# Half-width one-hots in two halves of a bank, a ring of seven pairs for gathered rows, and a reordered opening

## The reference, cut to what matters

```
xn  = layernorm(x)
msg = relu(xn[src] + edge_attr @ W_edge + b_edge)        # 50000 x 256
agg = segment_sum(msg, dst, 3125)                        # dst is sorted
h   = (1 + eps) * xn + agg
g   = relu(batchnorm(relu(h @ W1 + b1) @ W2 + b2))
m   = linear_attention(xn; Wq, Wkv, Wproj)               # elu+1 features, 8 heads
x   = x + g + m
x   = x + mixture_of_experts(layernorm(x))               # 8 experts, top 2
```

## Time and profile before

| | us |
|---|---|
| time, median of 3 (lowest to highest) | 1177.69 (1177.09 to 1181.65) |
| span of the profiled execution (first to last instruction) | 1050.8 |
| what lies around the span, median less span | 126.9 |
| PE busy, share of the span | 964.7, 92% |
| DVE busy | 671.7, 64% |
| ACT busy | 513.5, 49% |
| POOL busy | 555.1, 53% |
| first and last gather issued | 44.2 and 545.8 |

### The profile page before, as it was taken

One profiled execution on the slowest core, in us unless ns is written; L12 is line 12 of the kernel. 1 busy time (PEld: TensorE's weight loads), 2 busy tenths in 40 slices (PEclk: granted clock), 3 DMA queues, 4 the chain that ended last, 5 costly groups with the idle time before them and its releaser, 6 DMA issues.

```text
span 1050.8 us, 17977 instructions
## 1 busy us (share of the span) xinstructions
PE 964.7 (92%) x5112; PEld 810.3 (77%) x5113; DVE 671.7 (64%) x1274; ACT 513.5 (49%) x1036; POOL 555.1 (53%) x627
## 2 busy tenths in 40 slices
PE   5898999999999999999998961799999999999994
PEld 4677888888888888877775860778888888888884
DVE  5455565656655565578886778666666666666663
ACT  3644555555454545455554566444444444444442
POOL 3277777777777777777760040224253353444442
PEclk8899999999999999999998986899999999999998
DMA  9667788788888878998762028412545636635321
GB/s 246 197 154 237 255 267 253 250 268 266 260 254 262 269 247 267 278 313 270 239 202 86 26 89 316 181 26 40 204 90 174 220 50 213 192 73 160 98 38 21
DMA packets 85472, 198.30 MB, mean 189 GB/s; under 512 B 19785, under 2 KB 37139, under 8 KB 84378
## 3 DMA queue, kind: packets, MB, share of 16 engines
q1 hardware_dynamic: 55926, 131.60, 36.1%
q0 software_dynamic: 28752, 64.45, 25.5%
q10 hardware_dynamic: 724, 1.42, 0.5%
HBM read 147.86 MB, written 49.97 MB: 188 GB/s over the span
## 4 chain that ended last, share of the span: by engine, by line
POOL 29%; PE 29%; DMA 19%; issue 13%; DVE 7%; ACT 2%; POOLq 1%; SPq 0%; DVEq 0%; ACTq 0%
POOL work L758 29%; DMA out<-work,rowc 11%; PE banks L1141 6%; PE banks L1166 4%; DMA work<-token_table,tokc 4%; PE banks L470 3%; PE banks L446 3%; PE banks L1168 2%; PE banks L969 2%; PE banks L1054 2%; PE banks L1151 2%; DMA work<-in_edge_attr 1%; PE banks L1042 1%; DMA wts<-in_src 1%; DVE st L1776 1%
## 5 line engine op out<-in xcount | busy, mean ns | idle before, releaser
L758 POOL DMA_INDIRECT work<-node_table,srcT x391 | 379.5, 971 | 157.0 <-issue 117.6
L470 PE MATMUL banks<-work 128*128 128x256 f32 x780 | 179.1, 379 | 1.1 <-issue 1.1
L446 PE MATMUL banks<-w_edge,eaT 128*128 128x256 f32 x780 | 179.3, 380 | 0.0
L470 PEld LDWEIGHTS banks<-work 128*128 128x128 f32 x780 | 148.0, 190 | 21.8 <-issue 1.8
L446 PEld LDWEIGHTS banks<-w_edge,eaT 128*128 128x128 f32 x780 | 143.4, 191 | 16.8
L1166 PE MATMUL banks<-wsplit,hidT_hi 128*128 x416 | 153.3, 408 | 2.1 <-DVE hidT_lo L1908 2.1
L529 DVE TENSOR_TENSOR work<-banks,work 128x512 f32<-128x512 f32 x195 | 126.8, 682 | 26.1 <-DMA work<-node_table,srcT 15.2
L1141 PE MATMUL banks<-wsplit,xeT_hi 128*128 x416 | 134.3, 404 | 2.8 <-DVE xeT_lo L1915 2.8
L483 ACT COPY wts<-banks 128x256 f32<-128x256 f32 x66 | 24.6, 372 | 228.8 <-PE banks L470 227.8
L811 POOL DMA_INDIRECT out<-work,rowc x52 | 83.4, 1605 | 82.2 <-ACT work L1441 45.6
L1168 PE MATMUL banks<-wsplit,hidT_lo 128*128 x416 | 116.8, 281 | 0.0
(11 more groups left out here) (263 smaller groups left out, 1555.2 us busy)
## 6 DMA issues: line engine op xcount, KB each, us to landing
wsplit<-split_table SPq DMA_DIRECT2D x8, 4096.0 KB, 15.3
work<-in_edge_attr SPq DMA_DIRECT2D x65, 384.0 KB, 4.6
wts<-in_L_ffn_W SPq DMA_DIRECT2D x64, 256.0 KB, 4.9
split_table<-raw_hi SPq DMA_DIRECT2D x64, 256.0 KB, 3.0
split_table<-raw_lo SPq DMA_DIRECT2D x64, 256.0 KB, 4.3
work<-node_table,srcT POOLq DMA_INDIRECT x391, 4.2
xs<-in_x SPq DMA_DIRECT2D x8, 560.0 KB
wts<-in_L_ffn_b SPq DMA_DIRECT2D x8, 512.0 KB, 4.0
```

The lines of the kernel that those rows point to most:

```text
L446: last = nc.tensor.matmul(b[:, k * DIM:(k + 1) * DIM], eaT[:, u, 2 * q + k], w_edge[:], start=True, stop=True)
L470: last = nc.tensor.matmul(bank[5][:, 0:DIM], onehot[:, u, j], msg[:, u, j], start=(j == 0), stop=(j == GT - 1))
L758: pool.indirect_dma_start(out=xg[n % NB][0:rows, j], out_offset=None, in_=node_table, in_offset=bass.IndirectOffsetOnAxis(ap=srcT[0:rows, ...
```

## The change

Three things are changed together.

**Opening.** The order of loads: SP loads chunk 0, the edge numbers, chunks 3 and 4 and the edge features of group 0; ACT's queue loads chunks 1 and 2, then `b_edge`, `Wr`, `eps` and `W_edge`. The weights of the attention, `W1`, `W2` and the edge features of group 1 are issued by SP after the stores of `node_table`. ACT loads the table of roots at its start. The moments go to POOL, in four rounds (`ROUNDS`: chunk 0; 1; 2; 3 and 4), and so do the additions of `b_edge` for chunks 0, 1 and 2, each into a stage of its own. DVE normalises chunk 4 itself and adds `b_edge` for chunks 4 and 3. The numbers `src` are turned first, those of `dst` after the transposes of x. POOL clears `hT` after its additions. The attention's weights are turned inside group 0 of the edge loop (`turn_weights`, `copy_weights`), before which DVE may not write the one-hots of group 0 and POOL may not issue the seventh pair of gathers. The transposes of x alternate between two sets of three banks.

**One-hots of 64 columns.** A group is two half groups of 384 edges; tile j holds edges of half j % 2. Each half has its own first node and a window of 64 nodes; the products of even tiles go to partitions 0 to 63 of the bank, those of odd tiles to 64 to 127. The window is added into `hT` in two instructions, `add_first` and `add_second`.

**Ring.** The gathered rows go into seven buffers of one pair each; pair i waits for the sum of pair i-7.

The diff, cut to its core (the slices for a second run, declarations of semaphores and the asserts are left out):

```diff
-        xg_work = view(work, 1536, 2, GT, DIM)
-        xg = [xg_work[:, 0], xg_work[:, 1]]
+        xg = [view(work, o, 2, DIM) for o in (1536, 2048, 2560, 3072, 3584, 4096, 8448)[:RING]]
-        onehot = view(work, 7680, 2, GT, P)
+        onehot = view(work, 7680, 2, GT, WINDOW)
...
-            rows = a["edge_attr_128"][bass.ds(g * GROUP, GROUP), :].rearrange("(p j) d -> p (j d)", j=GT)
-            sp.dma_start(ea[:, u].rearrange("p j d -> p (j d)"), rows).then_inc(ea_in[u], 16)
+            rows = a["edge_attr_128"][bass.ds(g * GROUP, GROUP), :].rearrange("(s p j) d -> p s (j d)", s=2, j=PAIRS)
+            sp.dma_start(ea[:, u].rearrange("p (s j) d -> p s (j d)", s=2), rows).then_inc(ea_in[u], 16)
...
         def aggregate(pe, n, u, fresh=False):
-                last = nc.tensor.matmul(bank[5][:, 0:DIM], onehot[:, u, j], msg[:, u, j], start=(j == 0), stop=(j == GT - 1))
+                half = slice(j % 2 * WINDOW, (j % 2 + 1) * WINDOW)
+                last = nc.tensor.matmul(bank[5][half, 0:DIM], onehot[:, u, j], msg[:, u, j], start=(j < 2), stop=(j >= GT - 2))
...
         def mark_window(dve, g, u):
-            nc.vector.tensor_tensor(onehot[:, u], iota_f[:].unsqueeze(1).to_broadcast([P, GT, P]),
+            wide = [P, GT, WINDOW]
+            nc.vector.tensor_tensor(onehot[:, u], iota_f[:, 0:WINDOW].unsqueeze(1).to_broadcast(wide),
...
+        def add_nodes(dve, n, u):
+            for q in range(PAIRS):
+                i = PAIRS * n + q
+                dve.wait_ge(e_ready, i + 1)
+                dve.wait_ge(xg_in[i % RING], 32 * (i // RING + 1))
+                nc.vector.tensor_tensor(msg[:, u, 2 * q:2 * q + 2],
+                                        bank[2 + q][:].rearrange("p (k c) -> p k c", k=2),
+                                        xg[i % RING], ALU.add).then_inc(sums_done, 1)
...
+            w = hT[:, :, bass.ds(start, WINDOW)]
+            nc.vector.tensor_tensor(w, turned[:, 0], w, ALU.add).then_inc(agg_first, 1)
...
+        def add_second(dve, n, start):
+            dve.wait_ge(agg_first, n + 1)
+            w = hT[:, :, bass.ds(start, WINDOW)]
+            nc.vector.tensor_tensor(w, turned[:, 1], w, ALU.add).then_inc(agg_read, 1)
...
+            for c, ready, n in ((0, rows_pool, 1), (1, rows_pool, 2), (4, rows_dve, 1), (2, rows_pool, 3), (3, rows_dve, 2)):
+                sp.wait_ge(ready, n)
+                for d, s in node_rows(node_table, table_stage[c], c):
+                    sp.dma_start(d, s).then_inc(rows_stored, 16)
+            sp.dma_start(w_natural[:, 2:6], a["L0_mix_Wkv"].rearrange("(r p) c -> p r c", p=P)).then_inc(weights_in, 16)
+            load_edges(sp, 1, 1, 1, True)
...
+            def add_bias(c):
+                if c == 0:
+                    pool.wait_ge(small_in, SMALL_DMAS * 16)
+                pool.wait_ge(xn_ready, CHUNK_TILES * (c + 1))
+                nc.gpsimd.tensor_tensor(table_stage[c][0:TILE], xs[0:TILE, c * CHUNK_TILES:(c + 1) * CHUNK_TILES],
+                                        b_edge[0:TILE].unsqueeze(1).to_broadcast([TILE, CHUNK_TILES, DIM]), ALU.add
+                                        ).then_inc(rows_pool, 1)
+            for r in range(3):
+                moments(r)
+            add_bias(0)
+            moments(3)
+            for c in range(1, BY_POOL):
+                add_bias(c)
             nc.gpsimd.memset(hT[:], 0.0).then_inc(h_zero, 1)
...
-                if n >= NB:
-                    pool.wait_ge(sums_done, PAIRS * (n - NB + 1))
                 for j in range(tiles):
-                    pool.indirect_dma_start(out=xg[n % NB][0:rows, j], out_offset=None, in_=node_table,
+                    i = PAIRS * n + j // 2
+                    if j % 2 == 0 and i >= RING:
+                        pool.wait_ge(sums_done, i - RING + 1)
+                    if j % 2 == 0 and i == 2 * PAIRS:
+                        pool.wait_ge(wT_ready, 2)
+                    pool.indirect_dma_start(out=xg[i % RING][0:rows, j % 2], out_offset=None, in_=node_table,
...
+            def turn_weights():
+                pe.wait_ge(weights_in, WEIGHT_DMAS * 16)
+                pe.wait_ge(miss_known, 1)
+                for rb in range(2, 6):
+                    for k in range(HALVES):
+                        last = nc.tensor.transpose(bank[5 + k][:, (rb - 2) * P:(rb - 1) * P], w_natural[:, rb, k * P:(k + 1) * P],
+                                                   ident[:])
+                last.then_inc(wT_ready, 1)
...
+            stats_of(0).then_inc(stats_ready, 1)
+            scale_of(0)
+            stats_of(1).then_inc(stats_ready, 1)
+            stats_of(2).then_inc(stats_ready, 1)
+            dve.wait_ge(ids_in, 64)
+            nc.vector.tensor_copy(src_f, src_i).then_inc(rel_ready, 1)
+            scale_of(1)
+            stats_of(3)
+            scale_of(2)
+            stats_of(4).then_inc(stats_ready, 1)
...
+            scale_of(3)
+            normalise_x(4)
+            dve.wait_ge(small_in, SMALL_DMAS * 16)
+            add_bias(4)
+            add_bias(3)
```

More of the change, by code:

```diff
@@ L283, in build @@
         xn_ready = sem("xn_ready")
-        rows_ready = sem("rows_ready")
-        rows_stored = [sem(f"rows_stored{i}") for i in range(STAGES)]
+        xn_last = sem("xn_last")
+        rows_pool = sem("rows_pool")
+        rows_dve = sem("rows_dve")
+        rows_stored = sem("rows_stored")
         ids_memset = sem("ids_memset")
@@ L295, in build @@
         h_zero = sem("h_zero")
-        xg_in = [[sem(f"xg_in{u}_{q}") for q in range(PAIRS)] for u in range(NB)]
+        xg_in = [sem(f"xg_in{i}") for i in range(RING)]
         eaT_ps = sem("eaT_ps")
@@ L459, in aggregate_tail @@
             pe.wait_ge(msg_ready, PAIRS * (n + 1))
-            nc.tensor.matmul(bank[5][:, 0:DIM], onehot[:, u, 0], msg[:, u, 0], start=True, stop=True).then_inc(agg_ready, 1)
+            for i in range(2):
+                last = nc.tensor.matmul(bank[5][i * WINDOW:(i + 1) * WINDOW, 0:DIM], onehot[:, u, i], msg[:, u, 0],
+                                        start=True, stop=True)
+            last.then_inc(agg_ready, 1)
         def aggregate(pe, n, u, fresh=False):
@@ L659, in _ @@
             with sp.If(again > 0):
-                with sp.Fori(0, WINDOWS) as w:
+                with sp.Fori(0, PASSES) as w:
                     n0 = (w + 1) * GROUPS
@@ L1298, in copy_group, with copy_weights @@
                     copy_tail(act, n, n % 2)
+            def copy_weights():
+                act.wait_ge(wT_ready, 1)
+                for k in range(2):
+                    nc.scalar.copy(wkvT[:, k], bank[5 + k][:]).then_inc(wT_copied, 1)
+                act.wait_ge(wT_ready, 2)
+                for t, b in ((wqT, 5), (wpT, 6)):
+                    nc.scalar.copy(t[:], bank[b][:].rearrange("p (k c) -> p k c", k=2)).then_inc(wT_copied, 1)
             copy_group(0)
@@ L1661, in _ @@
             for n in range(GROUPS - 2, GROUPS):
-                add_window(dve, n, starts[n % GT], TILES)
+                add_first(dve, n, starts[2 * (n % GT)], TILES)
+                add_second(dve, n, starts[2 * (n % GT) + 1])
             round_low(dve, SPLITS - 1)
```

344 lines of the change are left out of this document (191 added, 153 removed).

## The result

The changed kernel takes 1213.34 us (median of 4, 1196.72 to 1218.70) where the kernel before took 1177.39 (1171.07 to 1181.65) on the same chip: ratio 1.0266, 95% interval 1.0179 to 1.0353. The kernel is slower, by 1.8 to 3.5%. 1162 and faster were forecast.

What follows compares the result with a forecast made beforehand. PE and POOL were taken to bind side by side, 1% apart. Opening 7.2, longer stream -1.4 and lag 9.4 gave 15.2 us: span 1050.8 to 1035.6, plus 126.9 around it 1162.5, said as 1162; 8-in-10 range 1150 to 1180.

Steps and rivals of the forecast that it cites:

- 1035.6, and with 126.9 around it 1162.5: Whole kernel: span falls from 1050.8 to 1035.6 us; 126.9 us outside the span stay, giving 1162.5.
- 15.17 us for two groups: Edge stage: PE's pace before the change, embed of group 32 to that of group 34.
- holds: Edge stage: gathers starting inside a DVE operation on working memory wait for its end; 15.1 us in all against 9.7.
- POOL binds everywhere: Edge stage: one-hots save PE 1.1 us a group, so PE needs 13.0 us for two groups, 14.4 late; POOL limits.
- rival 3: One-hots: changing array shape stops PE, 21 to 46 us over 65 groups; slower, about 1198 us; chance 0.12.
- the 5.5 us of waits go: Ring: POOL's 5.5 us of waiting for sums disappears, as a lagging DVE no longer stops POOL.
- added waits 0: Ring: the new waits, one per pair, stand in existing 0.305 us gaps; priced at 0, at most 6 us.
- gain 7.2: Opening: first gather at 37.0 us instead of 44.15, a gain of 7.2 us (4 to 9.7).
- POOL needs it only after twelve gathers, at 52: Opening: group 0's sum, with weights landing at 42 to 43 us, comes before POOL needs it, so costs nothing.
- `hT` is cleared, hidden behind the stores: Opening: POOL's clearing of `hT`, 5.55 us to 33.7, costs nothing if the stores take longer.
- lag: 18.2 us ... become 8.8: End of edge stage: time from the last gather's end to L1696 falls from 18.2 to 8.8 us, gaining 9.4.
- Rival 2: Opening gives nothing, with POOL's additions at 4 us or weights late; 8 us from the lag only, 1170 us; chance 0.07.

Runs made afterwards that it cites:

- c_before: The kernel before, unchanged, profiled and timed again: 1190.2 us, ratio 1.003.
- x_onehot: Kernel before plus the 64-column one-hots, with the old opening and no ring: 1193.5 us, ratio 1.008 to the kernel before.
- x_ring: Kernel before plus a ring of six pair buffers, with 128-column one-hots and the old opening: 1210.7 us, ratio 1.015 to the kernel before.
- s_after2: Changed kernel with two small POOL operations after each gather, gathers 1.51 us apart: 1211.9 us, ratio 1.030 to the kernel before.
- x_both: Kernel before plus 64-column one-hots and the ring of seven, with the old opening: 1204.6 us, ratio 1.023 to the kernel before.
- s_two: Kernel before with two small POOL operations after each gather, gathers 1.51 us apart: 1168.4 us, ratio 0.992.
- s_mid: Kernel before with one POOL operation of 112 columns after each gather, gathers 1.43 us apart: 1137.5 us, ratio 0.966.
- p_rows: Kernel before with half the rows of each gathered tile left out from group 2 on: 1230.3 us, ratio 1.029.
- p_pe: Kernel before with only two of the six tiles of each group multiplied by their one-hots on PE: 1173.9 us, ratio 0.985.
- e_wide: Changed kernel with 128-column one-hots again and a ring of six pairs: 1224.7 us, ratio 1.034 to the kernel before.
- the first trace: Profile of the kernel before on which the prediction rests: span 1050.8 us, while timed executions of that kernel gave 1177.

## Why the prediction was wrong

**The step that failed first** is in the last line of the sum, "1035.6, and with 126.9 around it 1162.5". The 126.9 us were taken to lie outside the span and to stay. They lie in the edge stage: 446.2 for 341.3 us from group 5 to 50, and group 64 starts at 684.6 for 548.3. Every term for the stage (15.17 us for two groups, holds, POOL's 1.251 us for a gather, a stream of 502.7) was worked out for a pace that the timed executions do not have. There two groups take 20 us, POOL waits 150.3 us for sums, and neither PE nor POOL binds by its own work. That gives the wrong level. The wrong sign is in the terms themselves: 7.2 us gained by the opening, nothing lost by ring and one-hots, 9.4 gained at the end; each of the first three costs time in the ratios above, and the lag at the end grew.

**"POOL binds everywhere", and the faster PE is harmless.** PE's saving is there (1.1 us a group forecast, 1.05 measured with both turns, 2.59 to 1.54), and the two additions take 0.28 to 0.29 each as forecast. The page "TensorEngine Tiling (Array Packing)" of the Trainium skill, "Key Properties", which was cited for rival 3, says that a change of mode drains the engine: a stop of 0.093 us at each turn agrees, and is under the 0.16 to 0.35 that rival 3 put it at. Yet the one-hots alone cost 0.8%. What the prediction named last as a way to be wrong came in: PE's clock falls in its new gaps. From 100 to 400 us it is 0.93 in c_before and 0.89 in x_onehot; PE is marked busy 232.7 us there for 252.6, with 1220 starts for 1199:

```profile
100.00:400.00 300.00, 232.74 (x1220) 169.54 (x1221) 128.05 (x262) 122.64 (x262) 180.36 (x184) 0.89 0.64 203
```

Of the two levels, 1.2 GHz holds in about 22% of that stretch in place of 14% (twice the missing clock). That this fall is the whole 0.8% is argued, not shown.

**Ring: "the 5.5 us of waits go", added waits 0.** There were 150.3 us to go, and none went: 154.4. In c_before and x_ring, gathers are 1.66 and 1.73 us apart on average; x_ring's 1.5% is shown, how the ring costs it is not. The added waits do have a price where POOL has small operations between its gathers (0.32 us, s_after2), but none shows at 1.25 us. I also looked at standstills, the time from 100 to 540 us in which PE, ACT, DVE and POOL start nothing for over 1 us. It is 20 us in c_before, 53 in x_ring, 60 in x_both and 50 in the changed kernel, and none in s_two and s_mid; but p_rows and p_pe have no ring and 57 and 51 us, and p_pe is the faster one. So the standstills prove nothing against the ring.

**Opening: gain 7.2.** The first gather goes out at 48.6 for 37.0 forecast, 5.6 later than in c_before. Right: small POOL operations 0.20 us (0.28 apart, 2.0 a round for 1.6), additions 2.89 for 2.7, late weights as a danger. Wrong, by size: the chain above, that is the last small load, landed at 19.3 where the numbers were there at 13.1, the products of ones, for the most part at twice the spacing of full clock (6.2), ACT's copies ahead of the last root (1.3), DVE and POOL locking each other out (5.0), SP's fixed order of stores. "POOL needs it only after twelve gathers, at 52" became 75.45: PE turned the weights late, and POOL stood 11.8 us before the seventh pair. I had put "`hT` is cleared, hidden behind the stores" to nothing, without asking what DVE does beside it.

**End: "lag: 18.2 us ... become 8.8".** It is 21.3 us (last gather over at 706.6, edges done at 727.9); in c_before it is 17.0:

```profile
727.92 0.27 DVE L1822 MEMSET eq<- 128x250 f32 x1 [0.55 <-issue]
```

**Rivals.** Rival 3 had the sign and a time of 1198, which is luck: its turns cost 0.19 us a group, less than the products save, and e_wide without them is no faster. Rival 2 (the opening gives nothing) looked at the right place and is too small: the first gather is 5.6 us later. The rival that was missing: a trace whose span is a tenth shorter than the times is not the execution that is timed.

**Open.** Why PE's signals come late while POOL issues gathers, and why not in the first trace; by what the ring costs 1.5% and the one-hots 0.8%; why the losses of the opening and of these two do not add; why s_mid gains most. Taking the gathers off POOL was not tried.

## What to carry to other kernels

Hold the profiled span against the times first; if they differ by much more than the others' few us, here 127, the pace of each stage is in doubt, and so is a sum over it. In a stage of five engines that wait for each other, relieving one or letting one run ahead can cost: test with work taken out (p_pe, p_rows) what the stage reacts to before tuning its parts. If POOL issues many gathers in a row and its waits for other engines are long, try some room between them, and count the waits that stand between them.

## What the hardware showed unexpectedly

- With gathers 1.25 us apart, PE's signals to other engines came 5 to 6 us late after 8 to 12 us of them, in both kernels but not in the first trace; with gathers 1.51 us apart hardly any was late. One added operation of 112 columns on POOL per gather took 3.4% off the whole kernel.
- With two small operations behind each gather, a wait for a semaphore that no late signal held up made the next gather start 0.32 us later (1.83 us for 1.51, s_two and s_after2); without them it cost nothing (1.25).
- A gather of 64 rows takes POOL 0.90 us, one of 128 rows 0.946: halving the rows saves almost nothing there.
- Two products into different halves of the columns start 0.006 us apart. Going from products of 128 columns to those of 64, or back, costs 0.093 us (0.309 us from start to start in place of 0.216).
